# A post-norm decoder layer on one core: head, slot and tail of all five engines in a new order

## The reference

```python
x = _layernorm(x + self_attention(x))           # 16 heads of 16, causal, scores with a mixing matrix per head
x = _layernorm(x + cross_attention(x, ctx, mask))   # keys and values from 375 context rows
x = _layernorm(x + ffn(x))                      # width 704, silu(gate) * up

def fp4_linear(x, w):                           # every linear map of the ffn
    xq = fp4_quant_dequant(x)                   # blocks of 16: divide by max/6, round to the FP4 grid, multiply back
    wq = fp4_quant_dequant(w)
    return jnp.einsum('bsk,nk->bsn', xq, wq)
```

## Time and profile before

| what | value |
|---|---|
| time, median of 3 runs | 675.13 us (674.81 to 675.4) |
| the profiled execution, its own time | 676.12 us |
| its span | 674.3 us |
| PE busy | 572.2 us, 85% |
| DVE busy | 537.2 us, 80% |
| ACT busy | 285.4 us, 42% |
| POOL busy | 235.5 us, 35% |
| mean granted TensorE clock | 0.948 |

### The profile page before, as it was taken

One profiled execution on the slowest core, in us unless ns is written; L12 is line 12 of the kernel. 1 busy time (PEld: TensorE's weight loads), 2 busy tenths in 40 slices (PEclk: granted clock), 3 DMA queues, 4 the chain that ended last, 5 costly groups with the idle time before them and its releaser, 6 DMA issues.

```text
span 674.3 us, 15980 instructions
## 1 busy us (share of the span) xinstructions
PE 572.2 (85%) x5410; PEld 360.8 (54%) x5410; DVE 537.2 (80%) x1443; ACT 285.4 (42%) x671; POOL 235.5 (35%) x312
## 2 busy tenths in 40 slices
PE   5876589799989898888989888887989898987875
PEld 3544255355655656565655655564656554544543
DVE  3498688775989979798988979566989887886784
ACT  2442155365345445344444545453444454434312
POOL 5352064352253505243341605242343516133100
PEclk9997699698999999899999989997999999998988
DMA  7566435354453535244452535353453525320000
GB/s 226 143 168 175 128 130 138 95 150 110 105 148 93 153 92 141 72 118 137 120 144 78 149 91 145 111 158 83 115 140 105 142 88 140 83 72 23 29 1 24
DMA packets 75808, 76.95 MB, mean 114 GB/s; under 512 B 13056, under 2 KB 67280, under 8 KB 75728
## 3 DMA queue, kind: packets, MB, share of 16 engines
q1 hardware_dynamic: 73488, 73.58, 40.0%
q10 hardware_dynamic: 2240, 2.35, 1.0%
HBM read 39.72 MB, written 27.00 MB: 99 GB/s over the span
## 4 chain that ended last, share of the span: by engine, by line
PE 40%; DVE 37%; issue 10%; POOL 5%; ACT 3%; DMA 2%; SPq 1%; DVEq 0%; POOLq 0%; ACTq 0%
PE misc L2251 14%; DVE junk L1447 5%; PE misc L2237 4%; PE score L2171 4%; PE prob L2185 4%; PE xpv L2226 3%; DVE qt L1359 3%; DVE qt L1363 3%; PE misc L2337 3%; DVE qt L1353 3%; DVE qt L1361 3%; DVE amax L1439 3%; DVE qt L1356 2%; POOL rstd L752 2%; PE prob L2180 2%
## 5 line engine op out<-in xcount | busy, mean ns | idle before, releaser
L1447 DVE CUSTOM_DVE_ANT_0 junk<-score,maskbias 112x375 bf16<-112x375 f32 x256 | 129.3, 543 | 57.1 <-PE score L2171 56.8
L947 ACT ACTIVATE xP<-prob 128x448 f32<-128x448 f32 (+1 forms) x192 | 95.2, 540 | 90.3 <-PE prob L2185 86.5
L2251 PE MATMUL misc<-wguT,xqT 128*128 128x352 f32 x224 | 81.7, 497 | 1.8 <-ACT xqT L907 1.1
L748 POOL TENSOR_TENSOR aattT<-anum,aden 128x224 f32<-128x224 f32 x16 | 10.6, 665 | 204.9 <-DVE aden L1486 196.1
L728 POOL TENSOR_TENSOR move_a<-mT,negeye 16x448 bf16<-16x448 f32 x64 | 63.5, 1014 | 48.5 <-ACT mT L907 48.5
L728 POOL TENSOR_TENSOR move_x<-mT,negeye 16x448 bf16<-16x448 f32 x64 | 61.2, 971 | 54.7 <-ACT mT L907 54.7
L752 POOL TENSOR_TENSOR rstd<-veps,half 128x1 f32<-128x1 f32 (+1 forms) x44 | 27.1, 621 | 108.1 <-DVE veps L1522 108.1
L2171 PE MATMUL score<-xK,xQ 64*128 64x375 f16 x256 | 45.6, 348 | 17.6 <-DVE xmax L1447 16.6
L2251 PEld LDWEIGHTS misc<-wguT,xqT 128*128 128x128 f32 x224 | 44.7, 206 | 25.0 <-issue 10.0
L2185 PE MATMUL prob<-move_x,shift_x 128*128 128x448 bf16 x192 | 54.8, 365 | 1.2 <-POOL move_x L728 0.9
L2226 PE MATMUL xpv<-xP,xV 128*32 128x112 f32 (+1 forms) x1536 | 54.5, 273 | 1.0 <-ACT xP L947 0.9
(11 more groups left out here) (157 smaller groups left out, 1094.2 us busy)
## 6 DMA issues: line engine op xcount, KB each, us to landing
xk_dram<-xk_parts SPq DMA_DIRECT2D x64, 192.0 KB, 3.2
xK<-xk_dram SPq DMA_DIRECT2D x16, 768.0 KB, 4.5
ctxT_s<-in_ctxT SPq DMA_DIRECT2D x15, 375.0 KB, 3.5
ak_dram<-ak_parts SPq DMA_DIRECT2D x64, 64.0 KB, 2.2
aq_dram<-aq_parts SPq DMA_DIRECT2D x64, 64.0 KB, 2.1
aK<-ak_dram SPq DMA_DIRECT2D x16, 256.0 KB, 3.0
aQ<-aq_dram SPq DMA_DIRECT2D x16, 256.0 KB, 3.7
xq_dram<-xq_parts SPq DMA_DIRECT2D x64, 64.0 KB, 2.1
```

The source lines that it names most:

```text
L947: act.activation(xP[0:KEYS[c], g % 2, c], prob[m][0:KEYS[c], 0:GH * S].rearrange("p (h q) -> p h q", h=GH), ACT.Exp).then_inc(probs.taken[ ...
L1447: dve.tensor_tensor_reduce(junk[:, m], score[m][0:S, 0:SC], maskbias[:], 1.0, -3.0e38, ALU.add, ALU.max, xmax[:, b.par, h:h + 1]).then_inc ...
L2251: mm = pe.matmul(misc[m][0:rows_, 0:cols], actT(c), weightT(c), start=(c == 0), stop=(c == DT - 1))
```

## The change

No call is added or taken away, and no shape or number changes. Only the order is new, on all engines: `ramp`, `slot` and `drain` of SP, POOL, ACT, DVE and PE, and the three lists of the `misc` banks. In the changed file the code of TensorE stands five lines lower, so L2180 of before is L2185 there.

```diff
-MISC_ORDER = ["v", "k", "q", "hT1", "hT0", "A.mT", "down", "X.xT", "gate0", "up0", "gate1", "up1", "K0", "A.o",
-              "V0", "K1", "V2", "V1", "X.o", "A.xT", "X.mT", "A.q"]
+MISC_ORDER = ["q", "k", "v", "hT1", "hT0", "A.mT", "down", "X.xT", "gate0", "up0", "gate1", "up1", "K0", "A.o",
+              "V0", "K1", "V2", "V1", "A.xT", "X.o", "X.mT", "A.q"]
...
@@ slot of SP
                 put_k(i, fr)
+                next_x(i)
+                next_ctx(i)
                 put_q(i, fr)
-                next_ctx(i)
+                next_xT(i)
                 spread(a, 0)
+                spread(p, 1)
+                get(fr, aq_dram, aQ, aq_out, aq_in, apv_done)
                 get(fr, ak_dram, aK, ak_out, ak_in, apv_done)
-                next_x(i)
-                get(fr, aq_dram, aQ, aq_out, aq_in, apv_done)
-                next_xT(i)
-                spread(p, 1)
                 put_xk(kv)
@@ slot of DVE, its end
+                invert(ct, 1)
                 ctxk_lo(i, kv, 0)
-                invert(ct, 1)
                 ctxk_lo(i, kv, 1)
                 if f:
-                    quant_h(i, f, 1, 2)
+                    quant_h(i, f, 0, 6)
+                    quant_h(i, f, 1, 4)
                 max_cross(i, c, 7)
...
@@ ramp of SP, its start
+                load_mask()
+                put_q(at[-2], at[0])
                 put_k(at[-2], at[0])
...
@@ ramp of DVE, its start
-                k_lo(at[-2], at[0])
+                masks()
                 mixed_bias()
                 q_lo(at[-2], at[0])
-                k_lo(at[-1], at[1])
-                q_lo(at[-1], at[1])
-                ctxk_lo(at[-1], at[0], 0)
+                k_lo(at[-2], at[0])
                 quant_weight(0, 0)
...
```

More of the change, by code:

```diff
@@ new lines, in ramp @@
+                put_xk(at[2])
+                put_x1(at[1])
+                put_xq(at[1], at[2])
+                get(at[2], xk_dram, xK, xk_out, xk_in, xpv_done)
+                get(at[2], xq_dram, xQ, xq_out, xq_in, xpv_done)
+                put_q(at[2], at[4])
+                put_k(at[2], at[4])
+                get(at[4], aq_dram, aQ, aq_out, aq_in, apv_done)
+                put_x1(at[2])
+                next_ctx(at[2])
+                get(at[4], ak_dram, aK, ak_out, ak_in, apv_done)
@@ L855, in slot @@
                     shifts(2, ft)
+                power(0, a)
                 shifts(0, a)
                 attend(ct, 1)
-                keep_x1(a)
                 diagonal(i, c, 0, True)
@@ L887, in drain @@
                 attend(at[14], 1)
-                keep_x1(at[15])
+                power(2, at[9])
                 power(1, at[12])
+                shifts(2, at[9])
+                attend(at[15], 1)
                 power(2, at[10])
                 shifts(2, at[10])
-                attend(at[15], 1)
                 power(1, at[13])
@@ L1808, in slot @@
                 k_lo(i, fr)
-                q_lo(i, fr)
-                max_self(i, a, 2)
-                max_self(i, a, 3)
                 if f:
@@ L1921, in drain @@
                 moments(at[14], at[15], 0, "A.o", 2)
-                gate_(at[14], at[10], 0)
+                quant_x(at[10], 7)
+                max_cross(at[14], at[14], 5)
+                residual_ffn(at[14], at[9])
+                invert(at[13], 1)
+                quant_x(at[10], 8)
+                xq_lo_(at[14], at[15])
                 max_cross(at[14], at[14], 6)
-                residual_ffn(at[14], at[9])
-                up(at[14], at[10], 0)
                 max_cross(at[14], at[14], 7)
-                quant_h(at[14], at[10], 0, 0)
```

1021 lines of the change are left out of this document (506 added, 515 removed), and 8 rows, old and new, of the table MISC_IN.

## The result

The changed kernel takes 648.69 us (median; 644.62 to 650.12) against 674.97 for the kernel before beside it: a ratio of 0.961, with a 95% interval of 0.956 to 0.966. The forecast was 648. That the total fits so closely is luck: the slots came out 17.1 us better than forecast and the head 16.5 us worse, with the other sign, and these two misses cancel. In this and all later medians and ratios, executions over 1.5% above a kernel's fastest are left out.

A forecast was written before the change was run, and what follows sets the result against it. A slot was taken as TensorE's work plus its four waits, mainly on VectorE, which shares a port lock with GpSimd. Slots -16.6, head -8 and tail -3 took the 674.3 span to 646.7, hence 648 us by the median, range 634 to 666.

The forecast's parts named there:

- The slots, -16.6: Ten slots together: 11.7 us from shorter TensorE waits and 4.9 from the clock, bounds +5 and -34.
- step is 4: TensorE's 2.01 us wait for xq at turn_xq in a slot; 1.0 of it was to remain.
- the 0.3: Added in a slot for turn_max, which TensorE now reaches earlier than the maxima.
- the 0.2 for a bank: What remains in a slot of TensorE's 0.42 us wait for a bank that VectorE empties, now at project_q.
- the rounding: Sum of a slot's waits raised from 2.5 to 2.7 us for score banks not followed.
- The clock term: Five slots lose 1.48 us each to a lower clock, 7.4 in all; two thirds, 4.9, regained.
- Waits 1 and 2: TensorE's slot waits: xq_parts, 0.87 to 0; xattT, 0.71, replaced by 0.4 for x1 and 0.6 for maxima, 1.0 together.
- The head, -8: Before the slots: 5 us of VectorE work moved into idle time, 3 from earlier cross scores; bounds +2 and -16.
- The tail, -3: After the slots: 3 of 4.4 idle us saved at eight pairs of cross scores, 603 to 615; bounds 0 and 4.4.
- The wait only moves: Rival, 28%: TensorE still waits 2.0 at turn_xq and the clock falls as now; 662 us.
- The operands arrive late: Rival, 7%: in slots, xQ for the cross scores lands late and holds TensorE's queue; 684 us at 5 us later.
- The order doesn't matter: Rival, 5%: idle time removed from TensorE comes back at the next instruction; 675 us, within 0.2%.

The follow-up runs named there:

- norm_behind_maxima: The changed kernel with layernorm and steps 0 and 1 of quant_x put back behind the last max_self in VectorE's slot; 674.14 us, ratio to before 0.999.
- last_maxima_first: The changed kernel with GpSimd's preparations waiting for masks() (638.87 us), plus the last max_cross put ahead of two quant_h steps in VectorE's slot; 644.64 us.
- slot_end_undone: The changed kernel with the end of TensorE's slot, and the same in MISC_ORDER, as before the change; 642.98 us.

## Why the prediction was right, and where it was wrong

**The slots, -16.6, measured -33.65.** The failed step is 4: "Behind the last `max_self` step 3 and perhaps 4 get through before `move_a` starts; the four left go one per POOL instruction". Steps 3 to 6 got through, and two were left. The trace of before held what was needed to see it:

```profile
342.50 1.15 DVE L1439 TENSOR_REDUCE amax<-score 112x4 f32<-112x448 f32 x2
...
344.95 0.42 DVE L1353 TENSOR_TENSOR qt<-x,qinv 128x256 f32<-128x256 f32 x1
```

From the end of the last `max_self` (343.65) to `move_a` (345.27) there is 1.62 us. In the changed kernel this gap is 1.46 (337.23 to 338.69). Steps 2 to 5 take 0.24, 0.42, 0.29 and 0.23 alone, together 1.18, and step 6 need only have begun. I knew that a step costs about 1.0 beside GpSimd and 0.3 ahead of it, but counted the steps ahead by eye instead of adding them up. And I didn't look for VectorE's idle time, which is what the norm's new place fills.

Over the ten slots TensorE's idle time fell by 26.5 us (41.54 to 15.07), where the forecast had 11.7; its busy time fell by 7.2, where the forecast had 4.9 for the clock. In a full slot the idle time was forecast at 2.7 and is 0.87: of this the 1.0 that I left at `turn_xq` is the largest piece, the others are the 0.3, the 0.2 for a bank, the rounding and 0.24 at wait 2. That `norm_behind_maxima` shows 2.71 is by chance so close: it is made up of other waits (1.88 and 0.76).

The clock term was about right: three of the five falls are gone, where two thirds were to go. Waits 1 and 2 had the right size (0, and 0.76 where I said 1.0, though none of it at `turn_x1`), but for a reason that fell: neither hangs on the part of TensorE's order that was undone. For wait 2 I also named GpSimd's `power(2)` and `shifts(2)`; no run undid those alone. And `keep_x1` does not hold `layernorm`, which starts 0.16 ahead of it.

**The head, -8, measured +8.46,** outside its bounds (+2 to -16). The step that failed is "12.9 us is free there". VectorE was idle for that long from 12 to 32, but GpSimd was busy for 10.08 us of the same stretch, and I applied the rule of one step per GpSimd instruction to the slot only. I weighed the masks' transfer, which costs 1.9 us of waiting, and not their place beside GpSimd, which costs 7 more (`masks()` lasts from 13.59 to 23.21 here, and from 13.31 to 15.78 with GpSimd still). The sign that I named, more than 7.10 busy from 12 to 32, came (11.71), but by this lengthening. The first cross scores, forecast for 62 to 65, are at 72.46, and at 64.72 with the masks mended, where they still didn't shorten the head.

**The tail, -3,** has about the right size (6.31 in the profiled pair, 2 to 3 at the same clock), but not at the place that I named. The eight pairs of cross scores take 11.72 us from the first to the last instead of 12.45 (575.05 to 586.77, and 600.96 to 613.41), so they gave 0.7 of the 3. Behind them the tail is 4.9 shorter (56.03 against 60.89), of which 3.6 is less busy time of TensorE, at a clock of 0.98 instead of 0.90.

**The rivals.** *The wait only moves* is true of each later edit (`last_maxima_first`, `slot_end_undone`) but not of the change. *The operands arrive late* never showed: no wait at `scores_cross` in a full slot. *The order doesn't matter* fell with the ratio of 0.961. The 0.2% that I gave for what a measurement can tell was too small: executions of the kernel before took 667.38 to 679.88 us, and the intervals of the ratios reach 0.4% to 1% to either side.

The Trainium skill's rule in "SBUF — State Buffer", section "SBUF: two separate sides", is one lock, held for a whole instruction. The 0.84 to 1.06 us of a step beside `move_a` agree with it, and so does L1416, which doesn't end while a memset runs. The rule doesn't say who comes next, so it gives no reason why L1416 waited for three memsets. My reading that the rule speaks against the change was wrong. An order can't make the two engines share, but it can use idle time of one to get ahead of the other.
